# Row maxima of an attention kernel: split as they lie and written as rows by transfers in 8-byte pieces, in place of a transpose on TensorE

## The reference

```python
def safe_softmax(s):
    m = jnp.max(s, axis=-1, keepdims=True)
    e = jnp.exp(s - m)
    return e / (jnp.sum(e, axis=-1, keepdims=True) + EPS)
...
q, k, v = split_heads(x @ Wq.T), split_heads(x @ Wk.T), split_heads(x @ Wv.T)
sim = jnp.einsum('bhid,bhjd->bhij', q, k) * scale
out = jnp.einsum('bhij,bhjd->bhid', safe_softmax(sim), v)
...
x = x + attention(_layernorm(x))
x = x + ffn(_layernorm(x))      # fp4_linear(silu(gate) * up)
```

## Time and profile before

| | |
|---|---|
| Runs | 1541.82, 1543.38, 1545.9 us; median 1543.38 us |
| Span of the profiled execution | 1542.1 us; no other time of this execution is given, so what lies around the span is not seen |
| PE busy | 1462.9 us, 95% |
| POOL busy | 1247.5 us, 81% |
| DVE busy | 1177.7 us, 76% |
| ACT busy | 1129.8 us, 73% |
| TensorE clock granted, mean share of the span | 0.987 |

### The profile page before, as it was taken

The page is one execution under the profiler, slowest core; times in us unless marked ns, Lnnn a source line. Parts: engine busy times, 40 slices in busy tenths (PEclk is TensorE's granted clock), DMA queues, the critical chain, the costliest instruction groups (busy, mean ns, idle before and its releaser), DMA issues.

```text
span 1542.1 us, 35223 instructions
## 1 busy us (share of the span) xinstructions
PE 1462.9 (95%) x13828; PEld 968.6 (63%) x13828; DVE 1177.7 (76%) x2048; ACT 1129.8 (73%) x2082; POOL 1247.5 (81%) x1358
## 2 busy tenths in 40 slices
PE   4999999999999999999999999999999999999965
PEld 2566666666666666666666666666666666666644
DVE  7777787777777878687787868788686877868677
ACT  3777777777777777777777777777777777777732
POOL 4888989878888888788888878888888888878952
PEclk9999999999999999999999999999999999999997
DMA  6111110101111111111111111101111111111000
GB/s 166 43 42 43 42 43 22 43 22 42 43 42 43 31 36 26 42 43 46 36 32 25 43 43 42 46 23 37 30 46 43 42 36 31 26 42 45 3 4 14
DMA packets 46661, 59.78 MB, mean 39 GB/s; under 512 B 8672, under 2 KB 21920, under 8 KB 46496
## 3 DMA queue, kind: packets, MB, share of 16 engines
q1 hardware_dynamic: 46336, 57.26, 15.8%
q10 hardware_dynamic: 160, 0.26, 0.1%
HBM read 4.80 MB, written 2.10 MB: 4 GB/s over the span
## 4 chain that ended last, share of the span: by engine, by line
PE 76%; DVE 17%; POOL 3%; ACT 2%; issue 1%; DMA 1%; SPq 0%; ACTq 0%; DVEq 0%
PE ob L621 24%; PE st L593 14%; PE st L595 11%; PE sm L574 9%; DVE negm L905 6%; PE mb L510 5%; PE mb L526 4%; PE mb L515 2%; POOL p_low L437 2%; PE mb L1177 2%; DVE xn L1151 2%; PE mb L521 1%; DVE qw L1069 1%; PE mb L1188 1%; PE mb L539 1%
## 5 line engine op out<-in xcount | busy, mean ns | idle before, releaser
L437 POOL TENSOR_TENSOR p_low<-probs 128x512 f16<-128x512 f32 x1024 | 1081.5, 1067 | 234.1 <-ACT probs L720 228.4
L720 ACT ACTIVATE probs<-st,lift,exp_scale 128x512 f32<-128x512 f32 x1024 | 793.0, 775 | 236.7 <-PE st L595 213.2
L905 DVE TENSOR_REDUCE negm<-sm 128x1 f32<-128x1024 f32 x508 | 617.8, 1216 | 130.4 <-PE sm L574 128.2
L593 PE MATMUL st<-q_hl,k_hh 128*128 128x512 f16 x1024 | 394.0, 385 | 2.3 <-DMA q_hm<-m_low 2.3
L595 PE MATMUL st<-q_hm,k_l 128*128 128x512 f16 x1024 | 388.7, 380 | 0.0
L621 PEld LDWEIGHTS ob<-v,p_low 128*128 128x128 f16 x4096 | 274.4, 97 | 123.0 <-POOL p_low L437 2.9
L621 PEld LDWEIGHTS ob<-v,probs 128*128 128x128 bf16 x4096 | 275.4, 97 | 120.7 <-ACT probs L720 0.5
L621 PE MATMUL ob<-v,p_low 128*128 128x129 f16 x4096 | 315.7, 219 | 2.7 <-POOL p_low L437 2.7
L621 PE MATMUL ob<-v,probs 128*128 128x129 f16 x4096 | 316.7, 219 | 0.2
L574 PE MATMUL sm<-k_hh,q_hl 64*128 64x512 f16 x508 | 196.9, 388 | 25.2 <-DVE negm L905 22.3
L574 PE MATMUL sm<-k_hh,q_hm 64*128 64x512 f16 x508 | 197.0, 388 | 0.0
(11 more groups left out here) (169 smaller groups left out, 1541.7 us busy)
## 6 DMA issues: line engine op xcount, KB each, us to landing
k_hh<-k_high SPq DMA_DIRECT2D x128, 128.0 KB, 2.3
k_l<-k_low SPq DMA_DIRECT2D x64, 128.0 KB, 2.3
q_hl<-q_high SPq DMA_DIRECT2D x64, 128.0 KB, 2.3
q_hl<-q_low SPq DMA_DIRECT2D x64, 128.0 KB, 2.4
q_hm<-q_high SPq DMA_DIRECT2D x62, 128.0 KB, 2.3
x<-x SPq DMA_DIRECT2D x4, 512.0 KB, 7.2
q_hm<-m_high SPq DMA_DIRECT2D x128, 1.0 KB
q_hm<-m_low SPq DMA_DIRECT2D x128, 1.0 KB
```

The costliest lines, as they stand in the source:

```text
L437: return pool.tensor_tensor(p_low[b][:, j, :], p, p.bitcast(BF16)[:, 1::2], ALU.subtract)
L593: pe.matmul(st[s % 2][:, :], k_hh[n][:, s * P:(s + 1) * P], q_hl[n][:, half * HALF:(half + 1) * HALF], start=True, stop=False)
L720: nc.scalar.activation(probs[k % 2][:, s, :], st[s % 2][:, :], ACT.Exp, bias=lift[:, 0:1], scale=exp_scale[:, head, pair:pair + 1]).then_i ...
L905: nc.vector.tensor_reduce(negm[k % 2][:, s // 2:s // 2 + 1], banks[:, :, :].rearrange("p a n -> p (a n)"), AX.X, ALU.max, negate=True).the ...
```

## The change

The "m" jobs leave the table, and with them PE's transposes and their use of the mb banks. ACT's `max_high` and DVE's `max_low` split negm as it lies, 128x4, out of SBUF into one tile `m_parts`, 128x2x4 in float16. Both stand first in slot 2 of each unit, ahead of the jobs there, so that of unit 3 moves from (3,4) to (3,2). ACT waits for the reduces itself.

The transfers now read 4 values (8 bytes) from each of 128 partitions and write them one behind the other into the row of q_hm. For the values to come out in the order of the queries, partition p must hold queries 4p to 4p + 3. So `scores` takes as its stationary operand every fourth query, beginning at s // 2, in place of 128 neighbouring ones.

```diff
-JOBS = [("k0", 0, (0, 1), (0, 2), (0, 2)), ("m", 1, (0, 1), (0, 2), (0, 2)), ...
+JOBS = [("k0", 0, (0, 1), (0, 2), (0, 2)), ("k1", 1, (0, 3), (0, 4), (0, 4)), ...
...
-        m_high = [sb(f"m_high{n}", [IT, P], F16) for n in range(2)]
-        m_low = [sb(f"m_low{n}", [IT, P], F16) for n in range(2)]
+        m_parts = [sb(f"m_parts{n}", [P, 2, IT], F16) for n in range(2)]
...
-                    for part, rows in enumerate((m_high, m_low)):
+                    for part in range(2):
                         sp.dma_start(q_hm[n][part:part + 1, half * HALF:(half + 1) * HALF]
-                                     .rearrange("a (t i) -> a t i", t=IT), rows[u][:, :]).then_inc(s_md[u], 16)
+                                     .rearrange("a (p t) -> a p t", t=IT), m_parts[u][:, part, :]).then_inc(s_md[u], 16)
...
-                    unit = JOBS[n][ON_PE][0]
-                    wait(pe, s_mx, 4 * (4 * (g - 1) + unit + 2))
-                    last = pe.transpose(bank[0:IT, 0:P], negm[(unit + 1) % 2][:, :], ident[:, :])
...
-                        t = half * IT + s // 2
+                        tokens = slice(half * HALF + s // 2, (half + 1) * HALF, IT)
...
-                            last = pe.matmul(banks[:, h, :], q_rows[rows, t * P:(t + 1) * P],
+                            last = pe.matmul(banks[:, h, :], q_rows[rows, tokens],
                                              k_hh[n][rows, h * 512:(h + 1) * 512], start=True, stop=True)
...
-                    nc.scalar.activation(m_high[(JOBS[m][ON_PE][0] + 1) % 2][:, :], bank[0:IT, 0:P],
-                                         ACT.Copy, scale=1.0 / MAX_UNIT).then_inc(s_mh, 1)
+            def max_high(g, k):
+                u, number = (k + 1) % 2, 4 * (g - 1) + k + 2
+                wait(act, s_mx, 4 * number)
+                nc.scalar.activation(m_parts[u][:, 0, :], negm[u][:, :], ACT.Copy, scale=1.0 / MAX_UNIT).then_inc(s_mh, 1)
...
+                        if s == 2 and (cur if k < 3 else nxt):
+                            max_high(g, k)
                         for n in jobs_at(ON_ACT, r, k, s):
...
-                    nc.vector.scalar_tensor_tensor(out=m_low[u][:, :], in0=bank[0:IT, 0:P], scalar=1.0 / MAX_UNIT,
-                                                   in1=m_high[u][:, :], op0=ALU.mult, op1=ALU.subtract).then_inc(s_mr, 1)
+            def max_low(g, k):
+                u, number = (k + 1) % 2, 4 * (g - 1) + k + 2
+                wait(dve, s_mh, number)
+                nc.vector.scalar_tensor_tensor(out=m_parts[u][:, 1, :], in0=negm[u][:, :], scalar=1.0 / MAX_UNIT,
+                                               in1=m_parts[u][:, 0, :], op0=ALU.mult, op1=ALU.subtract).then_inc(s_mr, 1)
...
+                        if s == 2 and (cur if k < 3 else nxt):
+                            max_low(g, k)
                         for n in jobs_at(ON_DVE, r, k, s):
```

More of the change, by code:

```diff
@@ L43 @@
 EXPONENT = 0x7F800000
-JOBS = [("k0", 0, (0, 1), (0, 2), (0, 2)), ("m", 1, (0, 1), (0, 2), (0, 2)), ("k1", 1, (0, 3), (0, 4), (0, 4)),
[1 row of a table removed]
+JOBS = [("k0", 0, (0, 1), (0, 2), (0, 2)), ("k1", 1, (0, 3), (0, 4), (0, 4)),
[1 row of a table added]
         ("q1", 1, (1, 1), (1, 2), (1, 2)), ("o0", 0, (1, 3), None, (1, 4)), ("x", 0, (1, 5), (1, 6), None),
         ("t1", 1, (1, 5), (1, 6), None), ("g0", 0, (1, 7), (2, 0), (2, 2)), ("h0", 0, (1, 7), (2, 0), None),
[1 row of a table removed]
[1 row of a table added]
         ("u0", 1, (2, 3), None, (2, 4)), ("h1", 1, (2, 3), (2, 4), None), ("w0", 1, (2, 3), (2, 4), None),
@@ L110, in runs @@
         return 2 <= r <= 2 * (B - 1) and r % 2 == 0
-    if name == "w":
-        return r == W_QUANT[int(JOBS[n][0][1])][0]
-    return cur if JOBS[n][ON_PE][0] < 3 else nxt
+    return r == W_QUANT[int(JOBS[n][0][1])][0]
 def job_before(r, n):
@@ L267, in taken @@
         def taken(m, g):
-            name, unit = JOBS[m][0], JOBS[m][ON_PE][0]
+            name = JOBS[m][0]
             c = int(name[1:] or 0)
@@ L284, in taken @@
                 return ffn.taken[name[0]], ffn_two(g, 1 if name == "x" else 2) + 1
-            if name[0] in ffn.taken:
-                return ffn.taken[name[0]], 2 * ffn_two(g, 2 if name[0] == "h" else 1) + c + 1
-            return s_mr, 4 * (g - 1) + unit + 2
+            return ffn.taken[name[0]], 2 * ffn_two(g, 2 if name[0] == "h" else 1) + c + 1
         x_t = x.rearrange("b (t p) d -> p b t d", p=P)
@@ L534, in job @@
                     last = ffn.job(pe, name[0], c, bank, ffn_two(r, 2 if name[0] in "hd" else 1), ident)
-                else:
-                    unit = JOBS[n][ON_PE][0]
-                    wait(pe, s_mx, 4 * (4 * (g - 1) + unit + 2))
-                    last = pe.transpose(bank[0:IT, 0:P], negm[(unit + 1) % 2][:, :], ident[:, :])
                 last.then_inc(mb_ready[JOBS[n][1]], 1)
@@ L694, in take @@
                     ffn.take_scalar(name[0], c, bank)
-                elif name[0] == "m":
-                    wait(act, mb_ready[JOBS[m][1]], ready)
-                    nc.scalar.activation(m_high[(JOBS[m][ON_PE][0] + 1) % 2][:, :], bank[0:IT, 0:P],
-                                         ACT.Copy, scale=1.0 / MAX_UNIT).then_inc(s_mh, 1)
+            def max_high(g, k):
+                u, number = (k + 1) % 2, 4 * (g - 1) + k + 2
+                wait(act, s_mx, 4 * number)
+                nc.scalar.activation(m_parts[u][:, 0, :], negm[u][:, :], ACT.Copy, scale=1.0 / MAX_UNIT).then_inc(s_mh, 1)
             def round_(g, r, q):
@@ L861, in take @@
                                                    op0=ALU.mult, op1=ALU.subtract).then_inc(s_lo, 1)
-                elif name[0] == "m":
-                    u, number = (JOBS[m][ON_PE][0] + 1) % 2, 4 * (g - 1) + JOBS[m][ON_PE][0] + 2
-                    wait(dve, s_mh, number)
-                    nc.vector.scalar_tensor_tensor(out=m_low[u][:, :], in0=bank[0:IT, 0:P], scalar=1.0 / MAX_UNIT,
-                                                   in1=m_high[u][:, :], op0=ALU.mult, op1=ALU.subtract).then_inc(s_mr, 1)
                 elif name[0] == "v":
```

## The result

The changed kernel takes 1557.09 us (median of 4 runs, 1556.28 to 1558.46) beside 1543.99 us of the kernel before (4 runs, 1541.82 to 1545.9): ratio 1.008, interval 1.0063 to 1.0097. It is 12.4 us slower where 11.6 us less were forecast. The profiled execution's span is 1554.5 us, against 1542.1.

What follows compares the result with a forecast made beforehand. PE was taken to bound even rounds, with the chain changing hands in odd ones. Transposes 14.1 less losses of 1.3 and 1.2 gave 11.6 us, so 1543.4 - 11.6 = 1531.8 us, range 1526 to 1540.

Steps and rivals of the forecast that it cites:

- Price of max_low: On DVE, first in slot 2: the new 128x4 instruction takes 0.15 us, 0.27 at the upper end.
- The strided load: Scores' stationary tiles reading every fourth f16, 508 pairs: load no slower, 0 us; upper end 51 us.
- rival (a): Scores' loads: the every-fourth-query load is slow; doubled it gives 1583 us, decides from 23 ns a pair; chance 12%.
- What the removal gives: On PE: 128 transposes of negm leave, 0.11 us each, so at most 14.1 us given back.
- the loss at (2,1): In 12 odd rounds with FFN work PE waits there anyway: 0.11 us each, 1.3 us, not gained.
- The place (3,5): PE's scores there wait for DVE's reduce of (3,3): 0.10 us a round, 12 rounds, 1.2 us lost.
- Transfers and SyncE hidden: SyncE's queue is never behind; 8-byte pieces land in 2.3 us plus up to 0.7, inside 5.6 us of cover.
- (b): Row transfers: 8-byte pieces kept on one DMA engine land late, near 3900 us; chance 4%.
- max_high under 0.25 us, no wait of DVE for ACT: Slot 2: ACT's instruction takes at most 0.25 us; no wait of DVE for ACT counted beyond max_low's 0.15 us.
- (c): DVE takes the savings in all 16 odd rounds, only even rounds gain, 7 us: 1536.4 us; chance 8%.
- (d): Nothing is lost and DVE's relief shortens its stalls, up to 2.9 us more: 1526.4 us; chance 10%.

Runs made afterwards that it cites:

- both prices undone: Changed kernel with the low part made by POOL and neighbouring queries in the scores' stationary tiles, exponent's factor times 2 to the -24th: 1538.83 us, ratio 0.9974 to before.
- POOL's version: Changed kernel with the low part subtracted on POOL instead of DVE, from an extra float32 copy made by ACT: 1539.5 us, ratio 0.9962 to before.

## Why the prediction was wrong

- **Price of max_low, the step that failed.** The prediction took 0.15 us from den and 0.27 from m_low on 4x128, since "its price is not in this trace". Both rows have at most one SBUF input: m_low's other one was the PSUM bank. The new form reads twice from SBUF and took 811 ns, where a reduction with one input takes 153. What was priced by size had to be priced by what runs beside it. The sum had 1.2 us for the instruction, with the place at (3,5); taking it off DVE is worth 18 us. The Trainium skill, "SBUF — State Buffer", section "Who interferes with whom", states it: an instruction of DVE with two SBUF inputs contends with a POOL instruction that reads SBUF, whoever comes first has the ports to its end, and a reduction is never affected. The traces agree on the wait (108 ends 16 to 22 ns apart) and on the reduction (135 to 159 ns). They don't bear it out for every POOL instruction: beside rstd, which reads SBUF by the program, max_low didn't wait. The trace of before had the sign too: xn on 128x128 takes 1068 ns, about as long as one p_low beside it (1.04 us).
- **The strided load, taken as 0.** It costs 16 ns, 8.1 us in all, well below the doubling of rival (a) and under its 23 ns. With this error alone the forecast would be 1531.8 + 8.1 = 1540 us, still faster than before; it is not what turned the sign. The rule from "Door 1: The DMA port swizzle" of the same page, two reads in a line of 16 bytes are enough, is contradicted for this load: at 8 bytes the load already rises, from 93 to 109 ns, and at 16 bytes it is 140, not doubled.
- **What the removal gives, 14.1 us.** Right where it can be seen alone: with both prices undone the even round takes 44.69 us, 0.42 less than before, where 0.44 was forecast. The odd round 17 gains 0.39, the other odd rounds 0.3 (or more, where the kernel before took 46.65 and not 45.93), where 0.33 was left after the loss at (2,1). In the changed kernel's even round 0.44 - 0.26 = 0.18 us should remain, and 0.09 did. That POOL's version lies 5.9 us under the kernel before (0.38% of 1544.89), where 14.1 - 8.1 = 6.0 would be, is in part luck: it lost 2.4 us in round 7 (48.80 for 46.44), and in four odd rounds it gained 0.7 us that the kernel before had lost by itself.
- **Where the time went.** The terms by experiment: -14.1 (transposes) + 8.1 (loads) + 18 (max_low on DVE) = 12, measured 12.4 of span. That they meet so closely is in part luck, for in the whole time the prices didn't add up above. The 18 are 11 for the wait that the reduction doesn't have, and 7 for the place in the odd rounds. By place, against the kernel before: rounds 0 to 3 -1.1 us, rounds 4 to 9 +10.0 (51.21 - 43.44 = 7.8 in round 4 alone), even rounds from 10 on -1.0, odd ones from 11 on +4.7, from round 32 on -0.2. The 7.8 us of round 4 are one meeting and the clock that fell during it.
- **The place (3,5).** Named rightly, its size was not. The reduce waits there behind L880 and the quantisation's L1067, 1.01 us each, and PE waits with it (the 1.01 us of L1067 were there before, those of L880 are new):

```profile
799.08 1.01 DVE L880 SCALAR_TENSOR_TENSOR m_parts<-negm,m_parts 128x4 f16<-128x4 f32 x1
...
800.32 1.01 DVE L1067 TENSOR_SCALAR qw<-qw 128x256 f32<-128x256 f32 x1
...
802.53 0.40 PE L564 MATMUL sm<-k_hh,q_hl 64*128 64x512 f16 x1 [0.83 <-DVE negm L901]
```

  0.83 us of wait, where 0.10 was forecast.
- **Transfers and SyncE hidden.** Right: no wait for them, and they land in 2.0 us where 2.3 plus up to 0.7 us was taken; (b) fell. The added packets took about 9 ns each, (16.9% of 1554.5 - 15.8% of 1542.1) x 16 / 34816, an estimate from the shares, not 84. That the earlier place of unit 3 gives cover was also right, and needed on POOL; on DVE the same place cost 7 us.
- **max_high under 0.25 us, no wait of DVE for ACT.** Right: 193 ns, 2.1 us in 3 cases.
- **The rivals.** (a) named the right term, at six times its price (100 ns against 16). (c) looked at DVE in the odd rounds, where 4.7 us were then lost, but only as a place where a gain is lost. (d) counted on DVE's relief, and got 103.8 us of max_low for 34.9 us of m_low. None asked what DVE shares with POOL, which is busy 81% of the span.

## What to carry to other kernels

Before an operation moves to VectorE, or from PSUM to SBUF inputs, count its SBUF inputs and look at what GpSimd does at that place. With two, its price was here the rest of GpSimd's instruction, and of all that followed it without a gap, however small the tile. A TENSOR_SCALAR on SBUF alone paid it too; a reduction, and an operation with one input in PSUM, did not. Price a strided stationary operand by a run at that very step, and multiply by the loads that nothing hides. A tuned list can stand on the edge of such a meeting, so 0.15 us of work ahead of it may cost 0.8.

## What the runs showed of the hardware

- A 128x4 instruction on DVE with both inputs in SBUF took 141 to 6808 ns, by what POOL ran; with one input in PSUM (4x128) it took 257 to 280 ns. POOL's rstd did not hold it up.
- A one-input TENSOR_SCALAR is affected too (0.27 or 1.07 us on 128x256, 0.42 or 3.63 on 128x22), a TENSOR_REDUCE of 128x4 was not (153 ns, 128 times); POOL loses as well where it comes second (1.20 for 1.04 us).
- Loads of 64x128 float16: 93 ns packed or by 4 bytes, 109 by 8, 140 by 16.
- 128 pieces of 8 bytes into one partition land in 2.0 us; with 1024 transfers of 2-byte pieces, these and the 128 KB ones of the same queue landed in 7.9 to 8.7 us.
- In round 4 the mean granted clock was 0.93, with PE idle for 5.4 us of 51.21; before, without the stall, it was 1.00.
